# Attention loop of a perceiver block: keys and values projected together, PSUM banks shared out anew, orders of four engines adapted

## The reference, cut to what is computed

```python
# x: 128 x 32 x 256, ctx: 128 x 257 x 256, 16 heads of 16
z = layernorm(x);  q, k, v = z @ Wq.T + bq, ctx @ Wk.T + bk, ctx @ Wv.T + bv
x = x + softmax(q k' / 4 + mask) v @ Wo.T + bo
z = layernorm(x)
dt = softplus(z @ Wdt + dt_bias); cumA = cumsum(A * dt)      # state space layer
norm = exp(cumA) * cumsum(exp(-cumA))
x = x + (Y[0] / norm) @ W_out.T                              # Y of batch 0 alone
z = layernorm(x)
x = x + top-2 of 8 experts (silu(z @ Wg) * (z @ Wu)) @ Wd, weighted by the router's gates
```

## Time and profile before

| what | value |
|---|---|
| median of 3 runs | 1529.26 us (1528.14 to 1529.8) |
| the profiled execution | 1529.16 us, its span 1527.2 us |
| PE busy | 1422.5 us, 93% of the span |
| DVE busy | 1125.5 us, 74% |
| ACT busy | 1000.9 us, 66% |
| POOL busy | 838.1 us, 55% |
| attention stage | from 0 to some 1000 us |
| experts stage | from some 1015 us to the end |

### The profile page before, as it was taken

One profiled execution on the slowest core, in us unless ns is written; L12 is line 12 of the kernel. 1 busy time (PEld: TensorE's weight loads), 2 busy tenths in 40 slices (PEclk: granted clock), 3 DMA queues, 4 the chain that ended last, 5 costly groups with the idle time before them and its releaser, 6 DMA issues.

```text
span 1527.2 us, 53971 instructions
## 1 busy us (share of the span) xinstructions
PE 1422.5 (93%) x15668; PEld 1294.9 (85%) x15669; DVE 1125.5 (74%) x3967; ACT 1000.9 (66%) x2482; POOL 838.1 (55%) x1401
## 2 busy tenths in 40 slices
PE   6969999999999999999999999649999999999997
PEld 5858888888888888888888888449999999999997
DVE  3647777777777777777777777557877787787775
ACT  4726766767766766766766676237777777677674
POOL 4514655655655655565565554226665666566554
PEclk9969999999999999999999999569999999999999
DMA  5302544554333343343343331425555555556554
GB/s 187 81 12 81 167 140 130 165 159 128 110 103 90 98 114 90 88 119 88 97 117 86 87 81 41 180 78 160 143 162 140 155 145 160 138 144 161 137 141 111
DMA packets 102009, 183.81 MB, mean 120 GB/s; under 512 B 19392, under 2 KB 61376, under 8 KB 101792
## 3 DMA queue, kind: packets, MB, share of 16 engines
q1 hardware_dynamic: 86272, 164.35, 35.2%
q0 software_dynamic: 15680, 18.76, 7.0%
HBM read 152.63 MB, written 31.13 MB: 120 GB/s over the span
## 4 chain that ended last, share of the span: by engine, by line
PE 72%; DVE 8%; issue 6%; ACT 2%; DMA 2%; POOL 1%; POOLq 1%; DVEq 0%; ACTq 0%; SPq 0%
PE m L412 12%; PE k L412 10%; PE y_p L1420 9%; PE v_p L412 9%; PE up_p L1420 8%; PE gate_p L1420 8%; PE sc L412 7%; PE pt L471 5%; PE ht_p L1459 3%; DVE dtv L976 2%; DMA par<-zbuf,gi 2%; ACT wd L735 1%; PE m L493 1%; PE z_p L1426 1%; DVE kT L868 1%
## 5 line engine op out<-in xcount | busy, mean ns | idle before, releaser
L735 ACT ACTIVATE wd<-wd,nmx 128x257 f32<-128x257 f32 x512 | 254.7, 499 | 100.6 <-DVE nmx L879 97.2
L879 DVE CUSTOM_DVE_ANT_0 wd<-sc,wd 128x257 f32<-128x257 f32 x512 | 187.3, 422 | 56.1 <-PE sc L412 45.8
L1622 POOL DMA_INDIRECT out<-par,oi x71 | 113.5, 1599 | 146.7 <-ACT par L1528 146.1
L1249 POOL TENSOR_TENSOR ctx_lo<-wd,ctx_hi 128x516 fp32r<-128x516 f32 x128 | 165.3, 1291 | 48.9 <-ACT ctx_hi L711 44.1
L711 ACT ACTIVATE wd<-pt 128x512 f32<-128x512 f32 x256 | 151.5, 592 | 57.9 <-PE pt L471 57.7
L471 PE MATMUL pt<-con,wd 128*128 128x128 f32 x1024 | 161.0, 280 | 3.0 <-ACT wd L735 0.7
L412 PE MATMUL k<-ctx_hi,wkh 128*128 128x256 f32 x512 | 158.2, 309 | 1.4 <-POOL ctx_lo L1249 1.4
L412 PE MATMUL v_p<-wvh,ctx_hi 128*128 128x256 f32 x512 | 158.0, 309 | 0.5 <-ACT y L711 0.5
L1499 ACT ACTIVATE uw_hi<-wu 128x1408 fp32r x71 | 98.3, 1385 | 85.1 <-PE up_p L1420 84.8
L1610 POOL COPY oi<-par 128x4 int32 x71 | 148.2, 2088 | 0.0
L1557 DVE TENSOR_TENSOR uw_lo<-wu,uw_hi 128x1408 fp32r<-128x1408 f32 x71 | 115.4, 1626 | 41.2 <-ACT uw_hi L1499 41.2
(11 more groups left out here) (197 smaller groups left out, 4662.2 us busy)
## 6 DMA issues: line engine op xcount, KB each, us to landing
dl<-d_low SPq DMA_DIRECT2D x71, 768.0 KB, 4.4
wd<-in_ctx SPq DMA_DIRECT2D x128, 258.0 KB, 2.8
wd<-in_mask SPq DMA_DIRECT2D x512, 32.1 KB, 1.8
wd<-in_wd SPq DMA_DIRECT2D x24, 256.0 KB, 3.0
d_high<-wd SPq DMA_DIRECT2D x24, 256.0 KB, 2.0
d_low<-wd SPq DMA_DIRECT2D x24, 256.0 KB, 2.3
wd<-d_high SPq DMA_DIRECT2D x8, 768.0 KB, 9.1
wg<-in_wg SPq DMA_DIRECT2D x8, 704.0 KB
```

The costliest lines, as they stand in the source:

```text
L735: nc.scalar.activation(pr[:, g, :], sm[:, g, :], ACT.Exp, bias=nmx[:, g:g + 1], scale=-1.0, accum_out=rsum[:, g:g + 1]).then_inc(exp_done, 1)
L879: V.tensor_tensor_reduce(sm[:, g, :], SC[g][:, 0:S], msk[:, b, :], -1.0, 3.0e38, ALU.add, ALU.min, nmx[:, g:g + 1]).then_inc(max_done, 1)
L1249: G.tensor_tensor(ctx_lo[:, b % 2], ctx[:, b], ctx_hi[:, b % 2].bitcast(F32), ALU.subtract).then_inc(lo_done, 1)
L1622: G.indirect_dma_start(outd[:, :], bass.IndirectOffsetOnAxis(oi[:, s, 1:2].bitcast(U32), 0), yb[:, s, :], None, compute_op=ALU.add).then_i ...
```

## The change

What it does:

- **Banks.** OT and RP move from SC[0] to the K bank, over the keys that have been read: `weigh_values` (n) now waits for `k_done` of batch n+2, and `project_k` (n+2) for the reading of the outputs of batch n-1 (`ou_done`, `rp_done`). The second half of `transpose_probs` goes to V_, over the values that have been read: it waits for `v_done` of n+2, `project_v` for `pt_done` of the step before. PT serves the first half alone. `px` gets two buffers.
- **PE's order.** `project_v` follows `project_k` directly; `turn_c` of a step moves behind the `scores` of the next one.
- **softplus.** Four of its temporaries lie in free columns of SC[1] in PSUM, with one operation more (`sp_y`, a second copy of y); `scores` of b = 1 wait for `a_done`. The chain's operations are put between `maxima`, `take_keys` and others instead of running in one piece; `select` is cut in five functions for the same purpose (their operations stay).
- **Orders of DVE, ACT and POOL** as the diff shows. `decays` goes to the next tile's b = 0, `keep`, `take_z2T` and `take_z3T` to the next step, `residual1` and `statistics2` from b = 0 to b = 1, `place` from b = 1 to b = 2.

The diff's core:

```diff
-        px = sb("px", [P, 2, NH, NG, 2])
+        px = sb("px", [P, 2, 2, NH, NG, 2])
...
-        OT = SC[0][:, SP:SP + NH * 2 * Q].rearrange("p (a h q) -> p a h q", a=NH, h=2)
-        RP = SC[0][0:2 * H, SP + NH * 2 * Q:SP + NH * 2 * Q + Q]
+        OT = K[:, 0:NH * 2 * Q].rearrange("p (a h q) -> p a h q", a=NH, h=2)
+        RP = K[0:2 * H, NH * 2 * Q:NH * 2 * Q + Q]
...
                 at_least(pe, k_done, 2 * n)
+                at_least(pe, ou_done, n - 2)
+                at_least(pe, rp_done, n - 2)
...
                 at_least(pe, v_done, n)
+                at_least(pe, pt_done, 2 * n - 2)
...
-                at_least(pe, ou_done, n - 1)
-                at_least(pe, rp_done, n - 1)
+                if b == 1 and runs(i - 2):
+                    pe.wait_ge(a_done, i - 1)
...
                 n = 4 * i + b
                 pe.wait_ge(exp_done, 4 * n + 2 * d + 2)
-                at_least(pe, pt_done, 2 * n + d)
+                at_least(pe, pt_done, 2 * n)
+                if d and runs(following(i, b)[0]):
+                    pe.wait_ge(v_done, n + 2)
...
-                        last = nc.tensor.transpose(PT[:, o:o + P], pr[:, g, t * P:(t + 1) * P], ident)
+                        last = nc.tensor.transpose((PT, V_)[d][:, o:o + P], pr[:, g, t * P:(t + 1) * P], ident)
...
-                if runs(nxt[0]):
-                    pe.wait_ge(max_done, 4 * n + 5)
+                if runs(following(i, b, 2)[0]):
+                    pe.wait_ge(k_done, 2 * n + 6)
...
-                mm(RP, px[:, :, :, :, :].rearrange("p k a g h -> p (k a g h)"), cst("sel")).then_inc(o_ready, 1)
+                mm(RP, px[:, b % 2].rearrange("p k a g h -> p (k a g h)"), cst("sel")).then_inc(o_ready, 1)
...
                     if runs(nxt[0]):
                         scores(*nxt)
+                    turn_c(*((i, b - 1) if b else (i - 1, TB - 1)))
                     if runs(two[0]):
                         project_k(*two)
+                        project_v(*two)
                     turn_a(i, b)
                     if runs(i):
                         weigh_values(i, b)
                     if runs(nxt[0]):
                         transpose_probs(*nxt, 0)
                     turn_b(i, b)
-                    if runs(two[0]):
-                        project_v(*two)
                     if runs(nxt[0]):
                         transpose_probs(*nxt, 1)
-                    turn_c(i, b)
...
-                copy(pT[:, 2 * d:2 * d + 2, :, :].rearrange("p g t n -> p (g t n)"), PT[:, :]).then_inc(pt_done, 1)
+                copy(pT[:, 2 * d:2 * d + 2, :, :].rearrange("p g t n -> p (g t n)"), (PT, V_)[d][:, :]).then_inc(pt_done, 1)
...
                     if runs(three[0]):
                         split_high(*three)
+                    if b == 2 and runs(i - 1):
+                        keep(i - 1)
                     if runs(nxt[0]):
-                        exponentials(*nxt, 0, 1, 2)
-                    if b == 1 and runs(i - 2):
-                        take_ynT(i - 2)
+                        exponentials(*nxt, 0)
+                    if b == 0 and runs(i - 2):
+                        decays(i - 2)
+                    if b == 2 and runs(i - 1):
+                        take_z2T(i - 1)
+                    if b == 3 and runs(i - 2):
+                        take_z3T(i - 2)
                     if runs(nxt[0]):
-                        exponentials(*nxt, 3)
-                    if runs(nxt[0]):
-                        take_probs(*nxt, 0)
-                    if runs(i):
-                        take_rp(i, b)
+                        exponentials(*nxt, 1, 2, 3)
                     if b == 0 and runs(i - 3):
                         gate_exp(i - 3)
                     if b == 0 and isinstance(i, int) and i == 2:
                         ssd()
-                    if b == 1 and runs(i - 1):
-                        keep(i - 1)
                     if b == 1 and k is not None:
                         piece_high(k)
-                    if b == 2 and runs(i - 1):
-                        soft_exp(i - 1)
-                    if b == 3 and runs(i + 2):
-                        take_z1T(i + 2)
+                    if b == 1 and runs(i - 2):
+                        take_ynT(i - 2)
                     if runs(two[0]):
                         take_values(*two)
                     if runs(nxt[0]):
+                        take_probs(*nxt, 0)
+                    if b == 3 and runs(i + 2):
+                        take_z1T(i + 2)
+                    if b != 0 and runs(i):
+                        take_rp(i, b)
+                    if runs(nxt[0]):
                         take_probs(*nxt, 1)
-                    if b == 1 and runs(i - 1):
-                        take_z2T(i - 1)
-                    if b == 2 and runs(i - 2):
-                        take_z3T(i - 2)
-                    if b == 3 and runs(i - 1):
-                        decays(i - 1)
+                    if b == 0 and runs(i):
+                        take_rp(i, b)
+                    if b == 2 and runs(i - 1):
+                        soft_exp(i - 1)
...
-            su, sr, sy, sw, ss = dtv[:, 2, :], dtv[:, 3, :], dtv[:, 4, :], dtv[:, 8, :], dtv[:, 9, :]
+            su, sy, sw = dtv[:, 2, :], dtv[:, 4, :], dtv[:, 3, :]
+            sr, sp_y, sp_sum, ss = (SC[1][:, SP + k * H:SP + (k + 1) * H] for k in range(4))
...
                 V.tensor_tensor(sy, su, ss, ALU.mult).then_inc(soft, 1)
+                V.tensor_tensor(sp_y, su, ss, ALU.mult).then_inc(soft, 1)
...
-                    dve.wait_ge(soft, NSOFT * j + 3)
-                    link(V.tensor_tensor(sw, sy, sy, ALU.mult), j, 4)
+                    dve.wait_ge(soft, NSOFT * j + 4)
+                    link(V.tensor_tensor(sw, sp_y, sy, ALU.mult), j, 5)
...
                     nxt, two = following(i, b), following(i, b, 2)
-                    if b == 3 and runs(i - 1):
+                    soft_now = b == 3 and runs(i - 1)
+                    pick_now = b == 3 and runs(i - 2)
+                    if runs(nxt[0]):
+                        maxima(*nxt, 0, 1)
+                    if soft_now:
                         softplus_ratio(i - 1)
+                    if runs(nxt[0]):
+                        maxima(*nxt, 2)
+                    if soft_now:
                         softplus_series(i - 1, 0, 1)
                     if runs(nxt[0]):
-                        maxima(*nxt, 0, 1)
+                        maxima(*nxt, 3)
+                    if b == 1 and runs(i - 1):
+                        residual1(i - 1)
+                    if b == 2 and runs(i - 2):
+                        normalise3(i - 2)
+                    if soft_now:
+                        softplus_series(i - 1, 1, 2)
+                    if runs(two[0]):
+                        take_keys(*two, 0)
+                    if soft_now:
+                        softplus_series(i - 1, 2, 3)
+                    if runs(two[0]):
+                        take_keys(*two, 1)
+                    if b == 1 and runs(i - 1):
+                        statistics2(i - 1)
+                    if b == 2 and runs(i - 3):
+                        place(i - 3)
+                    if soft_now:
+                        softplus_series(i - 1, 3, 4)
                     if runs(nxt[0]):
-                        maxima(*nxt, 2, 3)
+                        reciprocals(*nxt)
+                    if soft_now:
+                        softplus_series(i - 1, 4, len(ATANH))
+                    if b == 0 and runs(i + 2):
+                        statistics1(i + 2)
                     if b == 0 and runs(i - 1):
                         weigh(i - 1)
-                    if b == 2 and runs(i + 1):
-                        take_queries(i + 1)
-                    if b == 3 and runs(i - 2):
-                        take_logits(i - 2)
-                    if runs(two[0]):
-                        take_keys(*two)
-                    if runs(i):
-                        take_output(i, b)
-                    if b == 3 and runs(i - 1):
-                        softplus_series(i - 1, 1, len(ATANH))
-                    if b == 0 and runs(i - 1):
                         attention_out(i - 1)
                     if b == 1 and runs(i - 1):
                         normalise2(i - 1)
-                    if b == 2 and runs(i - 2):
-                        normalise3(i - 2)
-                    if b == 3 and runs(i - 1):
+                    if b == 2 and runs(i + 1):
+                        take_queries(i + 1)
+                    if pick_now:
+                        take_logits(i - 2)
+                    if soft_now:
+                        softplus_log(i - 1)
+                    if pick_now:
+                        select_top(i - 2)
+                    if soft_now:
+                        softplus_sum(i - 1)
+                    if runs(i):
+                        first_head(i, b)
+                    if pick_now:
+                        select_index(i - 2)
```

(46 more changed lines are left out.)

39 lines of the change are left out of this document (25 added, 14 removed).

## The result

The changed kernel takes 1515.54 us (median; 1514.07 to 1517.14) where the one before takes 1528.7 beside it: ratio 0.9914, 95% interval 0.9897 to 0.9931. It is faster, by 13 us and not by the 38.6 forecast, and 4.5 us above the top of the range. The profiled execution has a span of 1512.0 us against 1527.2, so 15.2 us are to be found in the two traces.

A forecast was written before the change was run, and what follows sets the result against it. The prediction took PE to bound the kernel. Its terms summed to -1.40 us a loop tile, times 25 = -35, with -3.6 for the written-out tiles: -38.6 on 1529.16, forecast 1490.5 us, range 1479 to 1511.

The forecast's parts named there:

- the written-out tiles: Six tiles outside the loop, without its turn: forecast to gain 0.6 us each, -3.6 in all.
- (a): End of step b = 3 on PE: the wait for `a_done` ahead of `sum_a` goes, gain 0.64 us a tile.
- (b): The loop's turn on PE, 0.56 us behind a wait, is partly hidden: gain 0.25 a tile, bounds 0 and 0.56.
- (c): PE's values right behind keys: first product 0.08 us shorter in three of four steps, gain 0.25 a tile.
- (d): Step b = 1: PE's loss to ACT's copy of `ynT` around `project_y` goes, gain 0.41 us a tile.
- (e): Step b = 3: PE's second transposes stall for ACT's `take_values`, cost 0.1 us a tile, bounds 0 and 0.4.
- (f): PE's weighing waits for both key halves of n+2 from DVE: covered, thinnest 0.2 us in b = 3, no cost.
- (g): Step b = 1: DVE's `normalise2` waits for POOL's `power`; nothing late in b = 2; cost 0.05 us, bounds 0 and 0.5.
- (h): Softplus on DVE: one more operation and PSUM operands, taken as 0 us; the skill's rule would add 0.65.
- the first: Rival: the loop's turn isn't hidden and the softplus chain ends late, -0.9 us a tile, 1504 us; chance 22%.
- rival 2: Slower: K bank ring of keys, weighing, heads and `take_rp`, with b = 1's POOL wait, delays PE; 1557 us; chance 8%.
- Rival 4: Better than summed: the loop's turn hidden wholly and no new stall, -1.8 us a tile, 1478 us; chance 10%.

## Why the prediction was wrong, point by point

The direction and most of the mechanisms were right; the sum per tile was 0.77 too good (25 x 0.77 = 19.2), the start 2.6, the written-out tiles 3.6, and what lies behind the tiles 2.0 the other way: 23.4, which is 1514.07 less 1490.5 within 0.2.

- **(a) right.** `a_done` was laid out at 6.25 after the scores. It comes at 445.33 + 0.16 against scores at 439.22: 6.27. The wait of the earlier trace rows is gone, 0.64.
- **(b) right in size.** Taken 0.25 of 0.56; 0.26 of issue is left, so 0.30 came. The reason given, that a wait for `v_done` keeps PE short of queued work, is what the four buffers show: without that wait the turn costs some 0.1. With `turn_c` moved in the kernel before, where PE doesn't wait there either, it costs nothing.
- **(c) gone in part.** Keys to values is 0.12 as said, and the values take 1.42 instead of 1.51. But only 0.09 is left in the balance of the tile for (c) and all that is not named. Second transposes cost 0.53 to 0.57 ahead of scores and not 0.44 as ahead of `project_out`; behind scores `project_out` costs 0.78 and not 0.95, `sum_a` 0.25 and not 0.34. I had priced what one product costs behind its new neighbour, and not what the move does to all the others. No run takes these apart.
- **(d) right**, 0.41.
- **(e) mis-sized.** ACT copies the values at 444.46, 5.24 after the scores, where I had 5.1, and PE stands 0.20, not 0.1; within the bounds of 0 to 0.4.
- **(f) failed.** I called 0.2 the thinnest cover and then costed it at nothing. In b = 3 DVE is through with the keys 4.38 after the scores, not 4.1 to 4.2, and PE could have started the weighing at 4.20 (443.66 less 0.24, less 439.22), not 4.4: two errors of 0.2 in a layout of 4 us, and the cover of 0.2 is a loss of 0.24 in every tile. Keys first doesn't mend it.
- **(g) the step that failed most.** Its mechanism came as written: DVE waits 1.58 us for POOL in b = 1, and the maxima of b = 2 start at 1.34, where I had 1.45:

```profile
431.08 0.41 DVE L1037 TENSOR_SCALAR z<-x,mv,rs 128x256 f32<-128x256 f32 x1 [1.58 <-POOL rs L1285]
```

  But "nothing is late" looked only at the user of the maxima. Behind them on DVE stand `normalise3`, the keys, `place` and `take_queries`, and PE needs the last: 0.37 instead of 0.05. The list of what is queued behind a waiting instruction ended a step too soon. Nor had it the 0.40 by which POOL's subtraction lengthens `normalise3`.
- **(h) right.** L980 in the changed kernel takes 173 ns with PSUM operands, three links 0.61 and six 1.45 before, so some 0.2 a link in place of 0.25. That is the earlier trace rows's 174 ns again. The some 65 ns more that the Trainium skill's table gives by my estimate (VectorE: DVE Perf Modes, the TRN2 errata) are contradicted by the measurement at 16 elements. What I missed is that the PSUM operands have a use of their own: without them the changed kernel would have been slower than before.
- **The written-out tiles failed**: 0 for -3.6. Behind the loop b = 1 and b = 3 took 6.92 and 6.43 before, so little was lost there; the changed kernel takes 7.26 and 6.56 to 6.88. And **the start** lost 2.6: there ACT sets the pace, and the second transposes, now in the values' bank, wait for its copy of the values in seven places. With four value buffers two are left, and the start is 3.4 us shorter:

```profile
31.43 0.63 PE L476 MATMUL v_p<-con,wd 128*128 128x128 f32 x4 [0.26 <-ACT wd L714]
```

  That wait I had placed in b = 3 of the loop alone.

By the balance of a tile: -0.64 (a) -0.30 (b) -0.41 (d) +0.20 (e) +0.24 (f) +0.37 (g) -0.09 for the rest, (c) with what it gave back, is -0.63. Of the 0.77 that the sum was too good, (g) has 0.32, (f) 0.24, (c) 0.16 and (e) 0.10, while (b) was 0.05 better. Of the rivals none came as told: the first has the nearest total (-0.9 a tile, 1504), but by a hidden turn that wasn't exposed and a chain that wasn't late. The ring of bank K, rival 2, was seen only as the 0.24 of (f). Rival 4 has a slip in its sum: 25 x 1.8 and the 3.6 give 1480.6, not 1478.

## What to carry to other kernels

When a change makes an in-order engine wait, write down everything that is queued behind the wait until the engine is idle again, across the step's end, and ask of each who waits for it; then treat a cover that is thinner than the error of your own layout as a cost. Put small operations that nobody waits for (`place` here) behind waits that exist anyway, and two-source operations from SBUF away from GpSimd's long ones, by a source in PSUM or by their place in the order.
